# Q's and K's squares made by ScalarE, and the first half's roots one step earlier, in an attention, state-space and expert kernel

## The reference, cut to what matters

```python
h = layernorm(x, ln_g, ln_b)
q = (h @ Wq).reshape(B, S, H, DH)      # 16 heads of 64; k and v the same way
q = l2norm(q) * q_scale                # x / sqrt(sum(x*x, -1) + eps)
k = l2norm(k) * k_scale
attn = softmax(where(causal, 10 * q @ k.T, -1e9))
out = (attn @ v).reshape(B, S, H * DH) @ Wo
h = layernorm(out)
gate = softmax(h @ gate_w + gate_b)    # 8 experts, all computed
moe = sum_e gate_e * (gelu(h @ w1_e + b1_e) @ w2_e + b2_e)
out = layernorm(moe)
```

## Time and profile before

| | |
|---|---|
| median of three runs | 1336.85 us |
| the profiled execution | 1335.85 us |
| its span in the profile | 1334.1 us |
| TensorE busy | 1157.3 us (87%) |
| VectorE busy | 1003.5 us (75%) |
| ScalarE busy | 739.8 us (55%) |
| GpSimd busy | 551.8 us (41%) |
| granted TensorE clock, mean | 0.93 |

### The profile page before, as it was taken

How to read it: one execution, slowest core, us unless ns; L and a number is a source line. 1 busy time by engine, 2 the same in 40 slices (tenths; PEclk the granted TensorE clock), 3 DMA queues, 4 the chain that set the end, 5 groups by cost and what they waited for, 6 DMA issues and landing times.

```text
span 1334.1 us, 27680 instructions
## 1 busy us (share of the span) xinstructions
PE 1157.3 (87%) x10435; PEld 951.6 (71%) x10435; DVE 1003.5 (75%) x2590; ACT 739.8 (55%) x1676; POOL 551.8 (41%) x468
## 2 busy tenths in 40 slices
PE   3675989797998979899897989979799897979977
PEld 1453778686876868688685867868587786858877
DVE  8569677787877778787777878778787877877652
ACT  3363656556465655746555574755647465565644
POOL 3472552707245280724618063361806337181100
PEclk9595989899998989999898998989899898999889
DMA  5001000000000000000000000000000000000000
GB/s 177 5 1 40 2 1 13 1 10 4 10 5 1 14 1 9 5 9 6 1 14 1 10 5 9 6 1 14 1 9 6 9 6 5 2 6 5 6 5 5
DMA packets 18723, 14.61 MB, mean 11 GB/s; under 512 B 2408, under 2 KB 16160, under 8 KB 18592
## 3 DMA queue, kind: packets, MB, share of 16 engines
q1 hardware_dynamic: 17680, 12.76, 3.3%
q10 hardware_dynamic: 912, 0.09, 0.0%
HBM read 10.75 MB, written 2.10 MB: 10 GB/s over the span
## 4 chain that ended last, share of the span: by engine, by line
PE 45%; POOL 25%; issue 17%; DVE 8%; ACT 3%; SPq 0%; DMA 0%; POOLq 0%; DVEq 0%; ACTq 0%
PE O L496 17%; POOL sq L801 10%; POOL nr L809 7%; POOL P L825 6%; PE J L341 4%; PE U L480 4%; PE U L481 4%; PE U L482 4%; PE S L359 3%; PE S L355 3%; POOL raw L817 3%; DVE st L1096 2%; DVE y L1106 1%; ACT L603 1%; PE O L412 1%
## 5 line engine op out<-in xcount | busy, mean ns | idle before, releaser
L825 POOL TENSOR_SCALAR_AFFINE_SELECT P<-P 128x512 f32<-128x512 f32 x128 | 84.2, 657 | 673.9 <-ACT P L666 672.5
L693 ACT ACTIVATE hid<-U,b1c 128x256 f32<-128x256 f32 x512 | 202.0, 474 | 202.0 <-PE U L482 200.8
L496 PE MATMUL O<-w2s,hid 128*128 128x128 f32 x2048 | 251.5, 276 | 0.0
L496 PEld LDWEIGHTS O<-w2s,hid 128*128 128x128 f32 x2048 | 238.5, 192 | 2.9
L412 PE MATMUL O<-Vx,P 128*128 128x66 f32 x1536 | 199.1, 280 | 9.1 <-ACT OT L672 9.0
L412 PEld LDWEIGHTS O<-Vx,P 128*128 128x128 f32 x1536 | 181.8, 192 | 24.1 <-issue 12.5
L1096 DVE TENSOR_TENSOR_SCAN st<-aexp,u 128x256 f32<-128x256 f32 x256 | 182.1, 711 | 4.4 <-ACT aexp L678 4.1
L809 POOL TENSOR_TENSOR nr<-nve,minus_half 128x32 f32<-128x32 f32 x32 | 177.3, 5541 | 2.7
L341 PE MATMUL J<-ident,raw 128*128 128x128 f32 x512 | 90.7, 328 | 96.1 <-POOL raw L817 62.5
L969 DVE TENSOR_REDUCE ssq<-sq 128x8 f32<-128x512 f32 x128 | 87.4, 683 | 91.3 <-POOL sq L801 91.0
L341 PEld LDWEIGHTS J<-ident,raw 128*128 128x128 f32 x512 | 71.2, 169 | 109.1 <-POOL raw L817 71.7
(11 more groups left out here) (160 smaller groups left out, 2138.7 us busy)
## 6 DMA issues: line engine op xcount, KB each, us to landing
xin<-in_L_attn_x SPq DMA_DIRECT2D x16, 128.0 KB, 2.2
xres<-in_L_attn_x SPq DMA_DIRECT2D x16, 128.0 KB, 2.6
hid<-in_L_ffn_w SPq DMA_DIRECT2D x2, 1024.0 KB, 6.1
out_dram<-fin SPq DMA_DIRECT2D x16, 128.0 KB, 1.8
raw<-in_L_ffn_Wq SPq DMA_DIRECT2D x1, 512.0 KB, 4.4
raw<-in_L_ffn_Wk SPq DMA_DIRECT2D x1, 512.0 KB, 6.3
raw<-in_L_ffn_Wv SPq DMA_DIRECT2D x1, 512.0 KB, 7.5
wos<-in_L_ffn_Wo SPq DMA_DIRECT2D x1, 512.0 KB, 11.0
```

Source lines behind the costliest of these rows:

```text
L496: last = mm(O[e % 2][:, t * P:(t + 1) * P], hid[:, e % 2, m, t * P:(t + 1) * P], w2s[:, e * FC + m, :], start=(m == 0), stop=(m == FC - 1))
L693: fn(hid[:, e % 2, f % FC, :], U[q % 2][:, m * SEQ:(m + 1) * SEQ], ACT.Gelu_apprx_tanh, bias=b1c[:, f:f + 1], scale=1.0 / WS).then_inc(gel ...
L825: nc.gpsimd.affine_select(out=diagonal, in_=diagonal, compare_op=ALU.is_ge, fill=0.0, base=0, pattern=[[0, 4], [1, P]], channel_multiplier ...
```

## The change

ScalarE's `copy_raw` is followed by an activation Square that reads the same bank J and writes `sq` directly; it waits first for the sums of the chunk two before, which used the same buffer, and it is the square, no longer the copy, that signals `qk_raw`. GpSimd's `square` and VectorE's squares in the prologue go away, and so does the semaphore `qk_sq`; `qk_sums` waits for `qk_raw`. On GpSimd `roots(i+1, 0)` stands in step 6 (the seventh), behind `select(i, 6)`, where it stood in step 7 behind `select(i, 7)` and the seventh square. Its units stay in steps 7 and 8.

```diff
             def copy_raw(s, j):
                 act.wait_ge(qk_ready, s * NJ + j + 1)
-                fn(raw[:, j, :], J[j % 2][:, :], ACT.Copy).then_inc(qk_raw, 1)
+                fn(raw[:, j, :], J[j % 2][:, :], ACT.Copy)
+                from_one(act, qk_sum, s * NJ + j - 1)
+                fn(sq[:, j % 2, :], J[j % 2][:, :], ACT.Square).then_inc(qk_raw, 1)
...
-            def square(s, j):
-                pool.wait_ge(qk_raw, s * NJ + j + 1)
-                from_one(pool, qk_sum, s * NJ + j - 1)
-                nc.gpsimd.tensor_tensor(sq[:, j % 2, :], raw[:, j, :], raw[:, j, :], ALU.mult).then_inc(qk_sq, 1)
...
                     if k < NP:
                         select(i, k)
-                    if new and k >= 1:
-                        square(i + 1, k - 1)
-                    if new and k == 7:
+                    if new and k == 6:
                         roots(i + 1, 0)
                     if new and k >= 7:
                         units(i + 1, 0, 2 * k - 14)
...
             def qk_sums(s, j):
-                dve.wait_ge(qk_sq, s * NJ + j + 1)
+                dve.wait_ge(qk_raw, s * NJ + j + 1)
...
                 for j in range(NJ):
-                    dve.wait_ge(qk_raw, j + 1)
-                    if j >= 2:
-                        dve.wait_ge(qk_sum, j - 1)
-                    V.tensor_tensor(sq[:, j % 2, :], raw[:, j, :], raw[:, j, :], ALU.mult).then_inc(qk_sq, 1)
                     qk_sums(0, j)
```

More of the change, by code:

```diff
@@ L184, in build @@
             g_vec g_act g_tr
-            qk_ready qk_raw qk_sq qk_sum n_const n_root unit t_ready t_hi t_lo v_ready v_done
+            qk_ready qk_raw qk_sum n_const n_root unit t_ready t_hi t_lo v_ready v_done
             m_ready mx_done mt_ready mt_done
@@ L195, in build @@
          g_vec, g_act, g_tr,
-         qk_ready, qk_raw, qk_sq, qk_sum, n_const, n_root, unit, t_ready, t_hi, t_lo, v_ready, v_done,
+         qk_ready, qk_raw, qk_sum, n_const, n_root, unit, t_ready, t_hi, t_lo, v_ready, v_done,
          m_ready, mx_done, mt_ready, mt_done,
```

## The result

The changed kernel takes 1355.92 us, the median of four runs (1352.86 to 1359.35); the kernel before, measured beside it, 1337.63 us. The ratio is 1.0138, with a 95% interval of 1.0121 to 1.0155: slower by 1.4%, where 1332 us had been forecast and 1356 was the upper end. The profiled execution is the slowest of the four, 1359.35 us with a span of 1357.6 us, against 1334.1 us before. So the traces differ by 23.5 us and the medians by 18.3.

What follows compares the result with a forecast made beforehand. TensorE was taken as the bound, through its stops and low clock. 14 x (-0.43 + 0.4) - 4.5 = -4.9 us, so 1335.85 - 4.9 + 1.0 = 1332 us, range 1316 to 1356.

Steps and rivals of the forecast that it cites:

- What bounds the kernel: TensorE, busy 87% of the span; winnable are its stops between 403 and 411 us and the low clock behind them.
- Part 1, the squares: Squares moved to ScalarE, 0.48 us each, hidden in ordinary steps; +0.4 us an iteration from full step 4.
- the rule that the prediction names: Trainium skill's advice to multiply on VectorE rather than ScalarE; by it squares would be 0.1 us dearer on ScalarE.
- Part 2, the roots: Roots in step 6: weigh(7) 2.2 us late after a 2.4 us stop, turn_qk(2) 0.43 us earlier.
- VectorE is not last, so 0: Fewer squares beside VectorE's scans shorten those scans, which was counted as 0 us.
- Part 3, the clock: Clock falls at weigh(7)'s stop, costing 2.9 us, and returns 2.5 later: net +0.4 us an iteration, between -2.5 and +3.8.
- The return: Half-speed work from 411.29 to 416.3 would regain 2.5 us, taken whole, if the clock fell earlier and was back.
- Once only: Savings outside the repeated iterations: prologue -2.0 us, body 0 -2.5 us, body 15 unchanged.
- The third: Clock low from weigh(7) to the stop before turn_qk(2), 3.8 us, nothing returned: 1380 us, 1355 in half the iterations; 30%.
- the first rival: The forecast itself: clock falls in step 8 and takes about what it returns, 1332 us (1326 to 1337); 40%.
- the second: Clock holds at weigh(7)'s stop or falls late and briefly: 1326 us, or 1314 to 1318 with some return; 20%.
- The sentence on the Trainium skill's rule for idle gaps: The skill warns only of longer idle gaps, so the clock would hold at weigh(7)'s stop, 1326 us; rows 9 disagree.

Runs made afterwards that it cites:

- e8: e7 with 7 spare matmuls ahead of turn_qk(1) and 6 ahead of turn_qk(2) in bodies 1 to 14; 1266.49 us, ratio 0.9472.
- e5: e3 with 15 more spare matmuls on TensorE ahead of turn_qk(2) in bodies 1 to 14; 1328.12 us, ratio 0.9936.
- e9: e5 with GpSimd holding back the second half's units until VectorE has made low parts 0 to 3, bodies 1 to 14; 1298.43 us, ratio 0.9705.
- e3: The changed kernel with 10 spare matmuls on TensorE ahead of weigh(7) in bodies 0 to 14; 1331.07 us, ratio 0.9941.
- e6: The kernel before with 12 spare matmuls ahead of turn_qk(1) and 9 ahead of turn_qk(2) in bodies 1 to 14; 1307.83 us, ratio 0.9784.
- e4: The changed kernel with the two V projections of step 8 moved ahead of weigh(7) on TensorE; 1302.90 us, ratio 0.9737.
- e7: The kernel before with squares on ScalarE, roots still in step 7, and the last eight decay exponentials spread later over steps 4 to 8; 1285.04 us, ratio 0.9607.
- e11: The changed kernel with 9 spare matmuls at the end of TensorE's prologue; 1353.54 us, ratio 1.0122.

## Why the prediction was wrong

**What bounds the kernel**: right. The stops between 403 and 411 us and the low clock behind them were the losses; e8, with its spare matmuls, has taken 4.7 us out of each body there.

**Part 1, the squares**: right. 0.48 us each in the stream, hidden in the ordinary steps, and 0.38 us a body in the full step where 0.40 was put. The wait on the sums ended nothing late: no idle time of ScalarE stands before any of the 128 squares. The Square takes 0.607 us, less than VectorE's 0.682; that the squares would be 0.1 us dearer on ScalarE by the rule that the prediction names rests on no row.

**Part 2, the roots**: right in its costs and in the path. `weigh(7)` 2.24 us later (2.2), a stop of 2.42 (2.4), `turn_qk(2)` 0.36 us earlier at a held clock (0.43). One term that it put at nothing was wrong: "VectorE is not last, so 0". The second half's units, which come earlier now, run beside VectorE's `scan(8)`; at a held clock that is a stop of 1.4 us at `gated_b2` (e5; it is gone in e9). In the changed kernel itself TensorE mostly comes there so late that the stop doesn't show; in bodies 4, 8, 13 and 14 it is 0.4 to 0.7 us long. I had costed the shorter scans of the heads' stage and not asked what the earlier units would run into.

**Part 3, the clock**: this is the step that failed. That it would fall at the new stop was right, it did in all 14 bodies. Both sizes were wrong. The cost of the fall I took at 2.9 us, with 3.8 as the full price. Over bodies 2 to 14 `turn_qk(2)` comes at 45.4 us on average, 3.35 later than in e3, where the clock holds, and at most 4.2 later. The low stretches in steps 8 and 9 are 3.4 to 10.2 us long; I had laid one of 6.8 us over the work. The return is the larger error: I took all 2.5 us, for a clock that is back up and stays up. From `turn_qk(2)` to `gated_b2` it is 5.5 us in the kernel before, 3.4 in e6, and 4.3 on average over those bodies of the changed kernel. The fall was worth 2.1 and 1.2 came back. In 7 of the 14 bodies the clock fell a second time behind the stop before `turn_qk(2)`, and in the four bodies named above the stop at `gated_b2` took a part. The sum by these sizes: -0.4 + 3.35 - 1.2 = +1.75 us, and the periods of bodies 2 to 14 give +1.77; I had 0.

The length of the stop before `turn_qk(2)` doesn't tell whether this second fall comes. It came in body 11 behind 3.09 us, and not in body 8 behind 3.40:

```profile
740.06 1.12 PE L341 MATMUL J<-ident,raw 128*128 128x128 f32 x7 [3.40 <-DVE QTl L975]
...
740.00:745.00 5.00, 4.57 (x39) 3.58 (x40) 4.96 (x10) 2.90 (x7) 1.74 (x2) 1.00 0.00 0
745.00:750.00 5.00, 5.00 (x50) 4.60 (x49) 2.94 (x7) 1.58 (x4) 0.00 (x0) 1.00 0.00 0
```

What decides it stays open.

**Once only**: the prologue's 2.0 is 2.09. Body 0 was put at -2.5 and is +1.2. Its second stage did get 5.4 us shorter (37.77 to 32.34), its first got 6.6 longer: 2.2 for the stop and the full step, and the rest is the clock again. It is low until 66.1 us where the kernel before had it up at 61.3, and it falls once more in step 8. Held against e4, where it was up at 58.3, the late rise costs 2.7 us by `weigh(5)`. Why it rose late in this execution is open, since its time varies by 12 us among runs with this prologue.

**The rivals.** The third, a clock low through steps 8 and 9 that returns nothing, is nearest: it had 3.8 us a body with no return, and 1355 us for half of the bodies. That number was met by luck: the mechanism was not "half of the bodies" but all of them, with a part returned, and a body 0 that gained nothing. The argument of the first rival, a period that clock and kernel settle between them, was half right: e3's bodies are 78.5 us as in the kernel before, although `turn_qk(2)` comes 0.36 us earlier. But in the changed kernel no such steady state was reached. Why the kernel before has one, and e7 a cycle of two bodies, stays open: no run was made to vary the period by itself. Nor was a version tried in which the power is split so that `select(7)` could go between its halves. One sum of the chances is wrong as well: half of the first case and the second are 0.40, not 0.44.

The sentence on the Trainium skill's rule for idle gaps (TensorE: Matmul & The Clock Gate, Why this matters for your kernels) stands corrected by the runs: a gap of 2.42 us, shorter than the gaps that it warns of, brought a fall 14 times out of 14 (12 out of 14 in e11), and filling it brought none; and 3.40 us before `turn_qk(2)` brought none in bodies 8 and 13 of the changed kernel and in bodies 1 and 2 of e4. On the table sets the page (ScalarE: Activation LUTs, Table sets) is borne out: there are 37 table loads in both traces.

## What to carry to other kernels

Before a long instruction of a slow engine is moved forward, look at what is queued behind it on that engine and who waits for that: here a mask of 0.64 us stood behind a power of 5.47 us, and it stopped TensorE, while the units behind the power were not read before some 11 us after it. Price a stop of TensorE by its idle time and by the clock that it may take from the work behind it, which here was far more than the 0.4 us a body by which the rest of the change was ahead; a few spare matmuls, or better the next real ones, put into the stop measure that price in one run. And a change of two parts is worth running as two: one was -3.4%, the other +3.5%.

## What the runs showed of the hardware that was not expected

- The clock's low stretches in step 8 had 3.4 to 10.2 us in bodies of equal work, and a body's length changed with them by up to 2.7 us (79.1 to 81.8 in bodies 2 to 13 of the changed kernel, 73.8 and 76.4 in turn in e7). The same stop of TensorE brought a fall in one body and none in another (e11, e4).
- A scan of VectorE beside GpSimd's two-input multiplies took 1.49 us instead of 0.68, and the two-input accumulation behind it 1.08 instead of 0.49 (e5, e9), while the low parts beside them, which read one operand from PSUM, took 0.47 us as without them (0.48).
- Square of 128x512 from PSUM on ScalarE took 0.607 us, the Copy of the same bank 0.59, and both hold the engine 0.48 us in a stream.
